# Attention and experts on one core: four turned buffers and split decay sums at the start, values in pairs, another order of small jobs, the state mask in PSUM, and row-by-row waits at the end

## The reference

```
xn = layernorm(x)
# branch 1: gated linear attention, 16 heads of 16, chunks of C = 128 tokens
q, k, v = silu(xn Wq'), silu(xn Wk'), xn Wv'
lf = cumsum over the chunk of log_sigmoid(xn Wf' + delta)          # 16 numbers a token
per chunk and head:
    o_inter = (q * exp(lf)) S
    A = (q k') * exp(lf_i - lf_j) below the diagonal, 0 above
    o = o_inter + A v
    S = exp(tot) * S + (k * exp(tot - lf))' v                      # tot = lf of the last token
s = rmsnorm(o) * norm_weight @ Wo'
# branch 2: experts choose tokens, 8 experts, the 128 best tokens of a batch each
aff = softmax(xn gate_w'); gating, idx = top 128 tokens of each expert and batch
x_e = (silu(xn[idx] w_gate') * (xn[idx] w_up')) w_down'
f = zeros; f[idx] += gating * x_e
out = x + s * silu(f)
```

## Time and profile before

| | us |
|---|---|
| median of 3 runs | 942.89 (942.76 to 942.97) |
| the profiled execution, its own time | 943.13 |
| its span from first to last instruction | 941.4 |
| PE busy in the span | 828.9 (88%) |
| DVE / ACT / POOL busy | 567.1 / 500.4 / 423.7 |

### The profile page before, as it was taken

The page is one execution under the profiler, slowest core; times in us unless marked ns, Lnnn a source line. Parts: engine busy times, 40 slices in busy tenths (PEclk is TensorE's granted clock), DMA queues, the critical chain, the costliest instruction groups (busy, mean ns, idle before and its releaser), DMA issues.

```text
span 941.4 us, 15773 instructions
## 1 busy us (share of the span) xinstructions
PE 828.9 (88%) x5640; PEld 673.1 (72%) x5640; DVE 567.1 (60%) x1033; ACT 500.4 (53%) x1153; POOL 423.7 (45%) x374
## 2 busy tenths in 40 slices
PE   2573389999999999999999999999999999999930
PEld 2442267888788878887888878887888788888820
DVE  6458246556655665566556665576557555565574
ACT  4552455456555665565546655665466555653421
POOL 5563451266525563457245714573356425460220
PEclk9866579999999999999999999999999999999975
DMA  8639894566755695668576757676677656764836
GB/s 273 233 111 215 292 216 153 155 156 158 199 158 143 164 210 154 165 151 174 164 169 166 155 182 179 144 170 181 166 136 167 181 163 187 167 123 141 251 88 203
DMA packets 132831, 163.89 MB, mean 174 GB/s; under 512 B 11792, under 2 KB 102416, under 8 KB 132624
## 3 DMA queue, kind: packets, MB, share of 16 engines
q1 hardware_dynamic: 119888, 145.00, 54.6%
q0 software_dynamic: 12288, 16.79, 10.9%
q10 hardware_dynamic: 576, 1.09, 0.3%
HBM read 117.48 MB, written 45.35 MB: 173 GB/s over the span
## 4 chain that ended last, share of the span: by engine, by line
PE 62%; POOL 9%; DMA 6%; DVE 6%; issue 5%; ACT 4%; SPq 3%; another core or an unknown queue 0%; ACTq 0%; POOLq 0%; DVEq 0%
PE g_ps L1296 15%; PE up_ps L1296 14%; PE y_ps L1322 14%; PE a_ps L1264 4%; PE o_ps L1286 4%; POOL w_r L750 3%; DMA qk_dram<-qk_r 3%; PE m_ps L1219 3%; POOL ffn_dram L781 3%; PE m_ps L1227 2%; PE m_ps L1246 2%; DMA lb_row<-lb_tiles 2%; POOL xg L769 1%; SPq L646 1%; SPq L688 1%
## 5 line engine op out<-in xcount | busy, mean ns | idle before, releaser
L888 ACT ACTIVATE dec_both<-lb_row,neg_lb 128x128 f32<-128x128 f32 x512 | 163.8, 393 | 155.3 <-PE o_ps L1286 112.6
L1322 PE MATMUL y_ps<-w_r,hid_r 128*128 128x256 f32 x1536 | 206.6, 284 | 4.9 <-DVE hid_r L1184 4.9
L1296 PE MATMUL g_ps<-xgt,w_r 128*128 128x512 f32 x768 | 204.2, 401 | 5.5 <-DVE xgt L1019 3.0
L1296 PE MATMUL up_ps<-xgt,w_r 128*128 128x512 f32 x768 | 203.4, 400 | 0.0
L1322 PEld LDWEIGHTS y_ps<-w_r,hid_r 128*128 128x128 f32 x1536 | 194.8, 190 | 5.9 <-DVE hid_r L1184 5.1
L750 POOL TENSOR_TENSOR w_r<-w_raw,w_r 128x768 fp32r<-128x768 f32 x64 | 122.0, 1907 | 115.2 <-ACT w_r L908 115.0
L1170 DVE SCALAR_TENSOR_TENSOR sg<-sg,g_ps 128x512 f32<-128x512 f32 x128 | 87.6, 685 | 129.8 <-ACT sg L955 109.9
L1296 PEld LDWEIGHTS g_ps<-xgt,w_r 128*128 128x128 f32 x768 | 136.6, 190 | 30.4 <-issue 3.3
L1296 PEld LDWEIGHTS up_ps<-xgt,w_r 128*128 128x128 f32 x768 | 138.7, 189 | 26.1
L781 POOL DMA_INDIRECT ffn_dram<-y_sb,idx_all x64 | 101.6, 1587 | 83.6 <-DVE y_sb L1092 67.8
L1184 DVE TENSOR_TENSOR hid_r<-up_ps,hid_r 128x512 fp32r<-128x512 f32 x128 | 88.3, 690 | 84.1 <-ACT hid_r L968 66.4
(11 more groups left out here) (187 smaller groups left out, 833.2 us busy)
## 6 DMA issues: line engine op xcount, KB each, us to landing
lb_row<-lb_tiles SPq DMA_DIRECT2D x64, 512.0 KB
w_raw<-w_experts SPq DMA_DIRECT2D x64, 384.0 KB
qk_dram<-qk_r SPq DMA_DIRECT2D x32, 512.0 KB, 4.1
k_st<-qk_dram SPq DMA_DIRECT2D x96, 128.0 KB
arena<-qk_dram SPq DMA_DIRECT2D x192, 64.0 KB
x_all<-x SPq DMA_DIRECT2D x8, 512.0 KB, 10.0
xn_dram<-xn SPq DMA_DIRECT2D x8, 512.0 KB, 4.6
e_row<-lb_tiles SPq DMA_DIRECT2D x64, 64.0 KB
```

The lines of the kernel that those rows point to most:

```text
L888: ins = act.activation(dec[p][:, j, :], lb_row[t // 2 % 2][:, h % HH, :], ACT.Exp, bias=neg_lb[:, ch, h:h + 1])
L1296: mm = pe.matmul(bank[:, :], w_r[:, m, a, at:at + P], xgt[:, b, k, half * 512:(half + 1) * 512], start=(j == 0 and k == 0), stop=(j == len ...
L1322: mm = pe.matmul(y_ps[:, j, :], hid_r[p][:, a, j * P:(j + 1) * P], w_r[:, m, b, DOWN:DOWN + D], start=(m == 0 and q == 0 and j % 2 == 0), ...
```

## The change

The diff touches five things. (1) `normalise` has four `turned` buffers; for batches 4 to 7 DVE, and no longer ACT, copies the turned form out of PSUM, and ACT in exchange scales batches 6 and 7 alone; the order of ACT's list is new. (2) In the head of `mixed` the five first jobs go round three PSUM banks (`bank_of`), and the decay sums are made in two parts (`PART`): chunks 0 to 7 first, the other 24 beside the first loop steps. `lb_row` is asked for before the stacks, `rows(0)` comes a step later, and the zero writes move into steps 8 to 11 of the loop. (3) `values` handles two groups of four heads at once, in every second step, and `dec` is a ring of four. (4) The tables of small jobs: second "k" behind `gate`, "v" behind `down`, "x" parts 2 and 3 in steps 14 and 15, "u" one step or three later; the mask of the state is applied to the new term in PSUM ahead of the multiply-adds. (5) The four last scatters have a semaphore each, and `fetch_f` of a batch waits for its own.

```diff
+TURNED, KEPT = 4, 2
-        turned = (xg[:, :, :].rearrange("p t d -> p (t d)"), small)
+        turned = [xg[:, :, :].rearrange("p t d -> p (t d)"), small[:, :]] \
+            + [t[:, :, :].rearrange("p k n -> p (k n)") for t in (e_row, qs0)]
...
-    SHARED = range(3, B)
+    SHARED = range(3, 6)
...
+        def keep_turned(engine, b):
+            engine.wait_ge(t_done[b % 2], b // 2 + 1)
+            if b >= TURNED:
+                engine.wait_ge(l_done[b % 2], (b - TURNED) // 2 + 1)
+                if b - TURNED < KEPT:
+                    engine.wait_ge(kept_lo, b - TURNED + 1)
+                else:
+                    engine.wait_ge(xt_stored[b % TURNED], 16)
...
@@ ACT in normalise @@
+                roots(3)
                 act.wait_ge(w_in, 64)
                 act.activation(attn_w[:, HI, :, :, :], w_raw[:, 0:3, :, :], ACT.Copy).then_inc(w_hi, 1)
                 scaled(4)
-                roots(3)
+                keep(2)
                 scaled(5)
-                act.wait_ge(wo_scaled, KD)
-                act.activation(wo_r[:, HI, :, :], w_raw[:, 3, :, :], ACT.Copy).then_inc(w_hi, 1)
-                keep(2)
+                keep(3)
                 scaled(6)
-                keep(3)
                 scaled(7)
-                for b in range(4, B):
-                    keep(b)
@@ DVE in normalise @@
-                scaled(6)
+                dve.wait_ge(wo_scaled, KD)
+                dve.tensor_copy(wo_r[:, HI, :, :], w_raw[:, 3, :, :]).then_inc(w_hi, 1)
                 by_token(2)
-                scaled(7)
-                for b in range(3, B):
+                by_feature(3)
+                for b in range(4, B):
+                    keep_turned(dve, b)
+                    dve.tensor_copy(turned[b % TURNED].rearrange("p (k n) -> p k n", k=KD), t_ps[b % 2][:, :, :])\
+                       .then_inc(t_read[b % 2], 1)
+                    by_token(b - 1)
                     by_feature(b)
...
-    BESIDE_JOB = (1, 2, 2, 11)
+    BESIDE_JOB = (1, 1, 1, 13, 0)
     AFTER_GATE = {0: ("kt", 0, 0), 1: ("v", 0, 1), 2: ("u", 0, 0), 3: ("x", 0, 0), 4: ("kt", 0, 1),
-                  6: ("u", 0, 1), 7: ("x", 0, 1), 8: ("kt", 0, 2), 9: ("k", 1, 0), 10: ("u", 0, 2),
+                  6: ("x", 0, 1), 7: ("u", 0, 1), 8: ("kt", 0, 2), 9: ("k", 1, 0), 10: ("k", 1, 1),
...
+    PART = (slice(0, 2 * TPB), slice(2 * TPB, NT))
...
+        def bank_of(job):
+            n = order[job]
+            if n < len(FIRST):
+                return (m_ps, a_ps[:, :, :].rearrange("p h n -> p (h n)"), g_ps)[n % 3]
+            if job in (("x", 0, 0), ("x", 0, 1)):
+                return up_ps[job[2]]
+            return m_ps
+        def free_at(job):
+            n = order[job]
+            if n < len(FIRST):
+                return max(0, n - 2)
+            return n if bank_of(job) is m_ps else 0
...
@@ SP in mixed @@
-                for i in range(4):
+                for i in range(2):
                     store_part(0, i)
-                sp.wait_ge(lb_turned, 2)
-                sp.dma_start(lb_tiles.rearrange("(g t) h n -> (t h) g n", g=TPB), lbt[:, :, :]).then_inc(d_out, 16)
-                load_stacks(0)
+                store_lb(0)
+                for i in range(2, 4):
+                    store_part(0, i)
                 sp.wait_ge(d_out, 16)
-                sp.wait_ge(chain, 9)
+                sp.wait_ge(chain, CHAIN)
                 for n in range(2):
                     load_lb(n)
+                load_stacks(0)
                 load_rows(0)
                 load_stacks(1)
-                sp.wait_ge(zero_set, 1)
-                for n in range(B):
-                    sp.dma_start(zero_rows[:, n * TPB * D:(n + 1) * TPB * D],
-                                 y_sb[:, :, :].rearrange("p t d -> p (t d)")).then_inc(zeroed, 16)
                 for u in range(LAST):
+                    if u == 1:
+                        store_lb(1)
+                    if u == AHEAD:
+                        sp.wait_ge(zero_set, 1)
+                    if AHEAD <= u < AHEAD + B // 2:
+                        for n in range(2 * (u - AHEAD), 2 * (u - AHEAD) + 2):
+                            sp.dma_start(zero_rows[:, n * TPB * D:(n + 1) * TPB * D],
+                                         y_sb[:, :, :].rearrange("p t d -> p (t d)")).then_inc(zeroed, 16)
...
                 for n in range(F_EARLY):
                     store_out(n)
                 sp.wait_ge(dn_done, XS)
-                sp.wait_ge(scattered, 16 * TPB * 2 * E)
                 for n in range(F_EARLY, B):
+                    sp.wait_ge(last_out[n - F_EARLY], 16)
                     fetch_f(n)
@@ ACT in mixed @@
                 def decays(t):
-                    ch, g, p = t // NG, t % NG, t % 2
+                    ch, g, p = t // NG, t % NG, t % 4
                     act.wait_ge(masked, t // 2 + 1)
-                    if t >= 2:
-                        act.wait_ge(av_done, t - 1)
+                    if t == 2:
+                        act.wait_ge(head_tot, 2)
+                    if t == 3:
+                        act.wait_ge(topk, 3 * ROUNDS + 1)
+                    if t >= 4:
+                        act.wait_ge(av_done, t // 2 - 1)
...
                     if u + 1 < TS:
                         decays(u + 1)
+                    if u == 0:
+                        sums(1)
+                    if u == 1:
+                        sums_turned(1)
+                        gates_left(1)
+                        rows(0)
@@ DVE, advance @@
-                    dve.wait_ge(s_done, at)
+                    dve.tensor_tensor(new, new, pairs, ALU.mult).then_inc(s_step, 1)
+                    dve.wait_ge(s_step, (TPB - 2) * b + c)
+                    dve.wait_ge(m_read, order["u", b, c - 1] + 1)
                     for kk in range(KD):
                         ins = dve.scalar_tensor_tensor(
                             out=state[:, kk, :], in0=state[:, kk, :], scalar=exp_tot[:, kk, b * TPB + c:b * TPB + c + 1],
                             in1=new[:, kk, :], op0=ALU.mult, op1=ALU.add)
                     ins.then_inc(m_read, 1)
-                    dve.wait_ge(m_read, n + 1)
-                    dve.tensor_tensor(state, state, pairs, ALU.mult).then_inc(s_done, 1)
@@ PE @@
-                    pe.wait_ge(a_read, t + 1)
-                    for j in range(G4):
-                        pads = v_pad[:, c, kk * G4 + j, :, :].rearrange("p a d -> p (a d)")
-                        mm = pe.matmul(o_ps[2 * HD * j:2 * HD * (j + 1), kk * P:(kk + 1) * P],
-                                       pads[:, late * HD:late * HD + 2 * HD], dec[p][:, j, :],
-                                       start=(c == 0 and late == 0), stop=(late == 1), skip_group_check=True)
+                    pe.wait_ge(a_read, 2 * pair + 2)
+                    for late in range(2):
+                        for j in range(G4):
+                            pads = v_pad[:, c, kk * G4 + j, :, :].rearrange("p a d -> p (a d)")
+                            mm = pe.matmul(o_ps[2 * HD * j:2 * HD * (j + 1), kk * P:(kk + 1) * P],
+                                           pads[:, late * HD:late * HD + 2 * HD], dec[(2 * pair + late) % 4][:, j, :],
+                                           start=(c == 0 and late == 0), stop=(late == 1), skip_group_check=True)
...
-                    if 1 <= u <= TS:
-                        values(u - 1)
+                    if u % 2 == 0 and 2 <= u <= TS:
+                        values(u // 2 - 1)
                     if u < TS:
                         scores(u)
+                    if u == 0:
+                        sums(1)
+                    if u == 1:
+                        sums_turned(1)
```

370 lines of the change are left out of this document (217 added, 153 removed).

## The result

| | before | after |
|---|---|---|
| median, us | 942.88 (942.76 to 942.97, 4 runs) | 902.33 (902.06 to 906.21, 4 runs) |
| profiled execution, its span | 943.13, 941.4 | 906.21, 904.5 |
| PE busy in the span, us | 828.9 | 799.0 |

The ratio is 0.958, with a 95% interval of 0.9554 to 0.9606. The change saves 40.6 us; 26 were forecast, and the time lies 4 us under the low end of the range.

The account below looks back on a forecast made before the run. PE was taken to bound the six middle periods, 4.7 us idle in 592.0, leaving mainly head and tail to gain. 943.13 - 14.4 (head) - 4 (jobs) - 3 (pairs) - 5.4 (tail) + 1 (zero writes): 917, range 906 to 930.

Parts of the forecast that it names:

- Values in pairs: -3: Loop on PE: 64 of 128 steps no longer enter the values, 0.11 us each; -3 us, ends -7 and +3.
- Order of jobs, -4: Loop on PE: the 4.7 us idle before the last q job go; -4 us, ends -4.7 and +2.
- Mask in PSUM, 0: State's mask on DVE: 11.7 us come back to DVE, but PE was not waiting for them; 0 us.
- Rival two: DVE's 11.7 us at the masks lie on PE's path and pairs give the full 7.0: 907 us, chance 0.12.
- Normalise, -5.5: First part: ACT's 10.1 us of waits go, the part ends near 43.7 against 49.2; -5.5 us, ends -2 and -8.
- First jobs and search, 0: Head: later search start and less holding of DVE set equal, search ends at 81.6; 0 us, ends -2 and +3.
- Decay sums and zero writes, -8.9: Head behind the search: third block of weights lands about 103.9, first gate's reader at 114.9 instead of 129.30; -8.9 us.
- Zero writes in the loop, +1: Steps 8 to 11: the writes leave 2 us of backlog in front of weights; +1 us, ends 0 and +12.
- rival one: Zero writes collide with loads of weights where they stand now, giving back up to 12 us: 929; 0.20 together with rival four.
- Row-by-row waits, -5.4: Tail: batch 4's read back needs only the first scatter, starting near 916.0 instead of 921.50; -5.4 us, ends -3 and -6.
- Rivals three and four: Three: pairs stall PE, 961 us, chance 0.03. Four: head held by something else as long, 929, 0.20 together with rival one.

Follow-up runs that it names:

- singles_free: The changed kernel with values of one group in every step, 'u' 2 behind `gate` in step 10 and 'k' 1 behind `down`: 927.9 us, ratio 0.9841.
- fours_free: rows_late with all four groups of a chunk in every fourth step, ring of five, state's products in the free half of `o_ps`'s bank: 898.3 us.
- fours_early_ot: fours_free with zero writes spread, last state product in step 14, DVE's low half of the output ahead of the hidden rows' low half: 883.5 us.
- before_pairs: The kernel before with only values in pairs, the ring of four and the smallest moves of small jobs that pairs need: 940.9 us, ratio 0.9975.
- before_loop: The kernel before with values in pairs, the ring of four and the new tables; head, tail and mask as before: 912.5 us, ratio 0.9681.
- before_norm: The kernel before with only the changed `normalise`: 939.0 us, ratio 0.9941.
- no_split: The changed kernel without the split decay sums, the three banks for the first jobs and the mask in PSUM: 900.8 us, ratio 0.9540.
- rows_late: no_split with the next batch's `e_row` loads asked for in step 6 instead of step 2: 896.8 us, ratio 0.9503.
- fours: The changed kernel with all four groups of a chunk in every fourth step, ring of five, 'u' 1 and 2 behind `down`: 930.0 us, ratio 0.9854.
- singles: The changed kernel with values of one group in every step, ring of four and tables kept: 940.2 us, ratio 0.9972.

## Why the prediction was wrong

The forecast was 917 with a range of 906 to 930; 902.3 was measured. The order of importance was wrong: I put the gain into head and tail, and three quarters of it is in the loop.

- **"Values in pairs: -3" failed**, and it is the step that made the forecast wrong. The mechanism named, a change of shape, was right as far as it went; the size was not: I had priced only the entry, 0.11 us, and taken half of it, in case entering the scores cost the same, which it does not. The rest stood in the earlier trace rows unseen. One group's values take 0.36 us and the scores behind them 0.34, and I read both as the price of the work. singles_free, fours_free and fours_early_ot show that a burst has 0.15 us of its own, that the scores lose 0.10 behind it, and that with the entry this makes 0.37 a pair, 0.36 again for each burst that fours remove. In the steady part that is 2.94 x 6.9 = 20 us, and there are 18 more steps ahead of it. The two profiles of the pair say the same: 17.7 us less PE work over 48 pairs is 0.37 each. The sentence "no matmul goes" misled me: the matmuls stayed and their time did not. The rows name the values' tiles 128*32 between groups of 128*128 and 96*128. By the Trainium skill (TensorEngine Tiling (Array Packing), Key Properties) a change of the tiling mode, not of the tile alone, drains TensorE; I had not weighed that rule. The runs agree with it, 0.36 to 0.37 us for each burst that goes, on either side of the scores; the page has no price, and that the drain is the cause was not measured by itself.
- **Order of jobs, -4: right.** Idle PE of 0.8 us a period is 0.2 now, and that is the mask's: with the mask over SBUF none is left. It needs the pairs, and the pairs need it: before_pairs gains 2 us, before_loop 30.
- **Mask in PSUM, 0: wrong in sign.** It costs 0.4 us a period, some 3 us in all. I asked whether DVE has room and not how long the bank is held. The rule of the Trainium skill (SBUF — State Buffer, Who interferes with whom) is borne out as far as the length goes, 424 ns from PSUM against means of 604 and 1152 over SBUF. Rival two has the nearest number, 907. Its single masks of over 2 us are there, but PE did not wait for them, and its gain there is refuted; its other half, the full 7.0 for the entry of the pairs, was right and a third of what the pairs gave. So its number is near by luck.
- **Normalise, -5.5: right** (before_norm -5.6, traces of the pair 5.5 to 5.8), but in part by luck: DVE ends 1.7 us before the 43.7 of my walk, and the stores, which I had named as the next limit, set the end at 43.7. DVE's cast of `wo_r`, 512 columns, took 1.33 us beside POOL's subtractions,

```profile
30.47 1.33 DVE L381 CAST wo_r<-w_raw 128x512 fp32r<-128x512 f32 x1
32.36 1.21 DVE L386 COPY xg<-t_ps 128x1024 f32<-128x1024 f32 x1
```

  more than a copy of twice the width from PSUM. It too ended 0.28 us behind POOL's subtraction. One small copy later DVE was idle again, for PE, so it cost nothing that shows.
- **First jobs and search, 0: right for the time** as far as no_split tells, wrong for the search's end, 2.9 us earlier than I walked. Nothing on the path used it.
- **Decay sums and zero writes, -8.9: too large, and of its two parts one is empty.** The zero writes alone gave 6.3 us, the split sums, together with the new first jobs, nothing that can be measured. My walk through SP's queue had the right stations; it had the q scaling 2.0 us too early and the block's landing 1.1 us too short. What it missed is that the same stations, with the same `e_row` loads ahead of the weights, come out as early without the split (ACT takes the third block at 106.33 in no_split). rows_late shows that these loads were the next bound.
- **Zero writes in the loop, +1: right in size as far as is known;** no run has them away, and spreading them gave 1.4 us by the time and 1.7 in the ramp. Their collision with a block of weights, rival one, is there in one profile, 2.0 us of idle PE and a granted clock of 0.67 and 0.60 over the two groups behind it (2.30 and 2.52 us), and not in the next.
- **Row-by-row waits, -5.4: too large.** By the profiles 1.9 to 3.8. I took the read back's 3.94 us over unchanged, although three scatters now run beside it; it took 5.85 and 7.56. A slip in the same term, the first scatter's landing (911.37 + 3.76 + 0.7 is 915.8, not 915.5), changes nothing, since the read back was put at 916.0 all the same.
- Rivals three and four did not come: no PE waits for scores, and the head moved.

The sum with the measured sizes: 943.1 - 5.6 - 6.3 - 30.1 + 2.8 - 1.9 to 3.8 is 900 to 902. The parts add, within their intervals of about 2 us each. The miss would have been larger but for luck: the head and the tail were put some 4 to 6 us too high together, which hid a part of what the loop gave beyond my 7.

## What to carry to other kernels

When PE is busy to the last microsecond, its work can still get cheaper: compare the time from one group's start to the next one's for the same group in different company, and count the bursts of small matmuls, since gathering them saves a fixed price for each. A move that gathers work shifts when its inputs are needed; half of the saving or all of it goes if the producer's place and its PSUM bank are not moved with it. And price a wait by what holds the buffer, not by how busy the engine is.

## What the runs showed of the hardware

- A burst of values costs 0.15 us beside 0.21 a group of four matmuls: 0.36, 0.57 and 1.01 us for one, two and four groups.
- An idle stretch of PE can cost twice, and need not. Behind each of the six idles of 2.34 us in fours the granted clock, the last but two column of these rows, fell to the lower of its two levels (1.2 GHz of 2.4), and the next group took 2.90 instead of 1.54 us; behind 1.40 us in the same kernel it stayed at 1.00. In singles six idles of 2.14 us stand in the same place of their periods: behind two of them the clock fell (2.77 instead of 1.60 us), behind four it did not.

```profile
352.68:355.20 2.52, 2.52 (x13) 2.52 (x13) 1.29 (x2) 0.00 (x0) 0.00 (x0) 0.50 0.62 167
```

```profile
321.46:324.19 2.73, 2.73 (x8) 2.15 (x8) 0.80 (x2) 0.00 (x0) 2.56 (x2) 0.51 0.91 306
351.20:352.60 1.40, 1.40 (x8) 1.14 (x7) 0.57 (x1) 1.20 (x4) 0.75 (x1) 1.00 0.04 15
```

- The same DVE instruction, 128x256 with both inputs in SBUF, takes 424 to 426 ns or, beside a computing instruction of POOL over SBUF, lasts until 0.27 to 0.29 us behind that one's end, up to 2.65 us. With one input in PSUM it took 422 to 426 ns beside the same POOL instruction too. A mean (1152 and 604 ns in two orders of work) hides this.
- Reading back 512 KB takes 3.9 to 4.0 us with the scatters landed and 5.4 to 7.6 beside three of them. The last two scatters, with read backs beside them, then land 6.3 to 8.0 us after their issue instead of 3.8 to 4.3.
